# Layer 0 scoring of a two-layer graph network: one gather per super-tile of 256 edges instead of one per visit

## The reference, cut to what matters

```
key_e = k_rel[edge_type, edge_src]
val_e = v_rel[edge_type, edge_src]
att = (q[edge_dst] * key_e).sum(-1) * rel_pri[edge_type] / sqrt(64)
seg = edge_dst * 6 + edge_type
w   = exp(att - segment_max(att, seg)) / segment_sum(..., seg)
hsum = segment_sum(w[:, :, None] * val_e, seg)
```

## Time and profile before

| | |
|---|---|
| device time, median of 3 runs | 4169.86 us (4167.93 to 4179.78) |
| profiled execution, first to last instruction | 4487.9 us, 50605 instructions |
| busy in the profiled execution | DVE 2869.6, PE 2636.7, POOL 2419.6, ACT 1640.2 us |
| TensorE clock granted, mean | 0.779 |
| scoring with its gathers, 569.5 to 1907.6 us | 1338.1 us |
| rest of scoring, 1907.6 to 2114 us | 206.4 us |
| sum of messages, 2114 to 2604.5 us | 490.5 us |

### The profile page before, as it was taken

The page is one execution under the profiler, slowest core; times in us unless marked ns, Lnnn a source line. Parts: engine busy times, 40 slices in busy tenths (PEclk is TensorE's granted clock), DMA queues, the critical chain, the costliest instruction groups (busy, mean ns, idle before and its releaser), DMA issues. The chain is left out here.

```text
span 4487.9 us, 50605 instructions
## 1 busy us (share of the span) xinstructions
PE 2636.7 (59%) x10364; PEld 1802.2 (40%) x10365; DVE 2869.6 (64%) x5456; ACT 1640.2 (37%) x4268; POOL 2419.6 (54%) x2361
## 2 busy tenths in 40 slices
PE   0499845555656565612888867734555546555553
PEld 0255423333333333302666655523444434443442
DVE  4544434578777877895888866634555555555557
ACT  2244322333433433341444435422333333333343
POOL 4322266677677667701444444446666666666651
PEclk9999967766676766655999989966776777777776
DMA  6366698888888888804777721134555555555552
GB/s 202 126 257 256 266 288 267 260 265 262 258 261 267 252 266 262 258 24 141 234 238 234 237 63 35 33 70 138 161 168 162 168 159 166 167 160 167 162 150 92
DMA packets 607757, 852.98 MB, mean 190 GB/s; under 512 B 158649, under 2 KB 501445, under 8 KB 600987
## 3 DMA queue, kind: packets, MB, share of 16 engines
q0 software_dynamic: 128272, 451.36, 32.6%
q1 hardware_dynamic: 466614, 386.90, 27.4%
q10 hardware_dynamic: 12686, 12.72, 0.9%
HBM read 560.70 MB, written 291.24 MB: 190 GB/s over the span
## 5 line engine op out<-in xcount | busy, mean ns | idle before, releaser
L1051 POOL DMA_INDIRECT rows<-kv,kvi x880 | 930.8, 1058 | 425.8 <-issue 256.4
L2224 POOL DMA_INDIRECT g_rows<-x1t,srci x880 | 842.1, 957 | 474.8 <-issue 240.6
L1127 PE MATMUL psD<-qs,hot 128*128 x1760 | 695.3, 535 | 497.5 <-issue 263.2
L1127 PEld LDWEIGHTS psD<-qs,hot 128*128 128x128 f32 x1760 | 418.8, 263 | 727.6 <-issue 671.0
L2378 PE MATMUL g_psM<-g_rows,g_hot 128*128 128x264 f32 x1760 | 622.4, 513 | 63.7 <-issue 31.8
L1339 DVE TENSOR_TENSOR prod<-rows,psD 128x512 f32<-128x512 f32 x440 | 300.2, 682 | 390.9 <-DMA hsort<-hrow,tposi 197.5
L2378 PEld LDWEIGHTS g_psM<-g_rows,g_hot 128*128 128x128 f32 x1760 | 423.6, 253 | 177.1 <-issue 76.8
L1211 ACT ACTIVATE off<-psB,npiota 128x256 f32<-128x256 f32 x440 | 206.7, 470 | 746.2 <-DMA hsort<-hrow,tposi 294.0
L1715 PE MATMUL psM<-wv,vhot 128*128 128x260 f32 x1760 | 430.7, 393 | 82.0 <-ACT wv L1664 58.5
L1715 PEld LDWEIGHTS psM<-wv,vhot 128*128 128x128 f32 x1760 | 322.7, 191 | 189.9 <-issue 81.4
L1634 POOL TENSOR_TENSOR wv<-vrows,wgt 128x1024 f32<-128x1024 f32 x110 | 231.8, 2107 | 285.7 <-DVE vhot L1743 210.8
(11 more groups left out here) (447 smaller groups left out, 4446.2 us busy)
## 6 DMA issues: line engine op xcount, KB each, us to landing
val_v<-rows SPq DMA_DIRECT2D x220, 512.0 KB
vrows<-val_v SPq DMA_DIRECT2D x220, 512.0 KB
sums_v<-g_run SPq DMA_DIRECT2D x110, 528.0 KB
g_drow<-drow_v SPq DMA_DIRECT2D x55, 512.0 KB
rows<-kv,kvi POOLq DMA_INDIRECT x880
g_rows<-x1t,srci POOLq DMA_INDIRECT x880
xs<-in_x ACTq DMA_DIRECT2D x12, 896.0 KB, 10.3
g_ndt<-nodeb SPq DMA_DIRECT2D x440, 6.0 KB
```

Source lines behind the costliest of these rows:

```text
L1051: nc.gpsimd.indirect_dma_start(out=rows[:, k], out_offset=None, in_=table, in_offset=bass.IndirectOffsetOnAxis(ap=index[:, i * SLOTS + k:i ...
L1127: nc.tensor.matmul(psD[:, 2 * (V % 2) + j, 0:D], hot[:, V % 2, j * P:(j + 1) * P], node[:, ds(blk[V % 4], 1)].rearrange("p o d -> p (o d)" ...
L2224: nc.gpsimd.indirect_dma_start(out=rows[:, i % NBUF, k, 0:ROW1], out_offset=None, in_=dr["x1t"], in_offset=bass.IndirectOffsetOnAxis(ap=v[ ...
```

## The change

The gathers and the value stores go by super-tile instead of by visit, in layer 0's scoring alone.

- `kvi` holds 784 columns of indices (two per super-tile), made from the sorted edges and no longer from the visits' records, which lose that field. POOL issues 784 gathers, two super-tiles (a *pair*, four slots) at a time: 196 pairs.
- The ring keeps 16 slots, now eight super-tiles. A visit finds its super-tile's seat by a register: DVE reads `seat_e` and `need_e` for four visits at a time (two register loads, eight assertions on the second one), waits until `need_e` pairs have arrived, and takes `rows` at the register's offset.
- SP counts the arrived pairs (`arrived`), stores the pair's values (196 stores), and two pairs later waits until the last visit of that pair is done, by a number read from `past_e`; then it counts it as free (`freed`). POOL waits for `freed` in place of `prod_done`. So POOL's pair n waits until pair n - 2 has landed.
- The transfers of the flags and of the scores out and back move from SP's loop to ACT's; the softmax steps start a tick later (LAG = 3).
- `sum_messages` loads each visit's two slots with a transfer of its own, from the super-tile's place: 440 transfers of 256 KB in place of 220 of 512 KB, with the block numbers read to registers.
- `prepare_edges` gains the steps that make the three tables, and SP's record stores fall from 24 to 20.

```diff
@@ edge_weights, POOL
-                for i in range(NI):
-                    for g in range(SLOTS // GS):
-                        if i:
-                            pool.wait_ge(prod_done, (i - 1) * (SLOTS // 2) + (g + 1) * (GS // 2))
-                            pool.wait_ge(kept[g], 16 * i)
-                        for k in range(g * GS, (g + 1) * GS):
...
+                for n in range(NG):
+                    i, g = divmod(n, GE)
+                    if i:
+                        pool.wait_ge(freed, n - GE + 1)
+                        pool.wait_ge(kept[g], 16 * i)
+                    for k in range(GS):
...
@@ edge_weights, SP
-                for n in range(NTICK):
-                    i, g = divmod(n, SLOTS // GS)
+                for n in range(NG):
+                    i, g = divmod(n, GE)
                     for k in range(g * GS, (g + 1) * GS):
                         sp.wait_ge(got[k], 16 * (i + 1))
+                    sp.sem_inc(arrived, 1)
                     o = dr["val"].rearrange("(i k p) d -> i p k d", k=GS, p=P)[n]
                     sp.dma_start(o, rows[:, g * GS:(g + 1) * GS, D:2 * D]).then_inc(kept[g], 16)
-                    if n % PT == PT - 1:
-                        flags(n // PT)
-                    if n >= PT and n % PT == 1:
-                        hand_over(n // PT - 1)
-                hand_over(NQ - 1)
+                    m = n - 2
+                    if 0 <= m < NG - GE:
+                        if m % 4 == 0:
+                            past = nc.values_load_multi_w_load_instructions(v["past_e"][0:1, m:m + 4], ...)[1]
+                        sp.wait_ge(prod_done, past[m % 4])
+                        sp.sem_inc(freed, 1)
@@ edge_weights, ACT
+                        if n % PT == PT - 1:
+                            flags(n // PT)
+                    if n >= PT and n % PT == 2 and n // PT <= NQ:
+                        scores_out(n // PT - 1)
+                    if n >= PT and n % PT == 3 and n // PT <= NQ:
+                        scores_in(n // PT - 1)
@@ edge_weights, DVE
-                    dve.wait_ge(got[k], 16 * (i + 1))
-                    dve.wait_ge(got[k + 1], 16 * (i + 1))
+                    if V % 4 == 0:
+                        dve.load(seats, v["seat_e"][0:1, V:V + 4])
+                        needs = nc.values_load_multi_w_load_instructions(v["need_e"][0:1, V:V + 4], ...)[1]
...
+                    dve.wait_ge(arrived, need_of[V % 4])
                     dve.wait_ge(dst_done, 2 * V + 2)
                     if V >= 2:
                         dve.wait_ge(sc_done, V - 1)
-                    tt(prod[:, b:b + 2], rows[:, k:k + 2, 0:D], psD[:, b:b + 2, 0:D], ALU.mult).then_inc(prod_done, 1)
+                    tt(prod[:, b:b + 2], rows[:, ds(seat_of[V % 4], 2), 0:D], psD[:, b:b + 2, 0:D], ALU.mult).then_inc(prod_done, 1)
@@ sum_messages, SP
+                        if g % 2 == 0:
+                            sp.load(regs, v["blk"][0:1, ds(i * V8 + 2 * g, 4)])
                         sp.wait_ge(wv_done[g % 2], i * (NG // 2) + g // 2 + 1)
-                        o = dr["val"].rearrange("(i k p) d -> i p k d", k=GS, p=P)[ds(i * NG + g, 1)]
-                        sp.dma_start(rows[:, g * GS:(g + 1) * GS], o.rearrange("o p k d -> (o p) k d")).then_inc(loaded[g], 16)
+                        for u in range(2):
+                            at = nc.s_assert_within(
+                                i * V8 + (2 * g + u) - sp.snap(regs[2 * (g % 2) + u], min_val=0, max_val=NB - 1), 0, NS - 1, ...)
+                            k = g * GS + 2 * u
+                            sp.dma_start(rows[:, k:k + 2], values[ds(at, 1)].rearrange("o p k d -> (o p) k d")).then_inc(loaded[g], 16)
```

More of the change, by code:

```diff
@@ L19 @@
 NT = NV // VT
+RE = 8
 NC = 2 * NV
@@ L36 @@
 EPS = 1e-5
+ROUND = 1.5 * 2.0 ** 23
 SLOPE = 0.2
@@ L410, in prepare_edges @@
         b128 = sb("b128", [P, VT])
-        rv = sb("rv", [P, VT, NF, SUP])
+        rv = sb("rv", [P, VT, NR, SUP])
         dq = sb("dq", [P, VT, SUP])
+        cmps = va[:].rearrange("p t s -> p (t s)")[:, 0:NS]
+        parts, whole, supf = (a[0:1].rearrange("p t s -> p (t s)")[:, 0:NV] for a in (va, vb, dq))
+        past = cmp[0:1, 0:NS]
         vrow = sb("vrow", [P, 3, VT, SUP], BF16)
@@ L559, in _, with whole_of @@
                 step(nc.vector.tensor_copy(v["blk"][:], bfull[0:1, :]))
+                step(nc.vector.scalar_tensor_tensor(out=past, in0=psum[0:1, 3, 64:64 + NS], scalar=1.0, in1=viota[0:1, 0:NS], op0=ALU.add, op1=ALU.add))
+                dve.wait_ge(s_pad, 16 * PADS)
+                step(nc.vector.tensor_copy(v["past_e"], past.rearrange("o (n k) -> o n k", k=2)[:, :, 1]))
                 step(tsc(b128[0:NT], bvt[0:NT], float(P), None, ALU.mult))
+                step(tt(supf, viota[0:1, :], bfull[0:1, :], ALU.subtract))
+                def whole_of(n):
+                    step(tsc(parts, supf, 1.0 / n, (n - 1) / (2.0 * n), ALU.mult, ALU.subtract))
+                    step(tsc(whole, parts, ROUND, None, ALU.add))
+                    step(tsc(whole, whole, ROUND, None, ALU.subtract))
+                for n, ring, seats, needs in ((2, RE, v["seat_e"], v["need_e"]),):
+                    whole_of(n)
+                    step(tsc(needs, whole, 1.0, None, ALU.add))
+                    whole_of(ring)
+                    step(nc.vector.scalar_tensor_tensor(out=parts, in0=whole, scalar=-float(ring), in1=supf, op0=ALU.mult, op1=ALU.add))
+                    step(tsc(seats, parts, 2.0, None, ALU.mult))
                 dve.wait_ge(s_got, 64)
@@ L956 @@
 NTICK = NI * (SLOTS // GS)
-STEPS, LAG = 43, 2
+STEPS, LAG = 43, 3
+NG = NS // 2
+GE = RE // 2
 PB = R // 2
@@ L1208, in _, with piece_rows, flags, scores_out @@
             def _(act):
+                def piece_rows(name, q):
+                    return dr[name][q * GR * PL:(q + 1) * GR * PL].rearrange("(g s) -> g s", s=PL)
+                def flags(q):
+                    if q:
+                        act.wait_ge(flags_free, q)
+                    for h in range(H):
+                        act.dma_start(fi[h * GR:(h + 1) * GR], piece_rows("first", q)).then_inc(f_in, 16)
+                        act.dma_start(la[h * GR:(h + 1) * GR], piece_rows("last", q)).then_inc(f_in, 16)
+                def scores_out(q):
+                    for n in range(2):
+                        t = 2 * q + n
+                        act.wait_ge(tr_out, t + 1)
+                        act.dma_start(dr["att"].rearrange("h (t c p) -> t c h p", c=PC, p=P)[t], stage[:, n]).then_inc(att_put, 16)
+                def scores_in(q):
+                    act.wait_ge(att_put, 32 * (q + 1))
+                    for h in range(H):
+                        act.dma_start(w[h * GR:(h + 1) * GR, q * PL:(q + 1) * PL],
+                                     dr["att"][h, q * GR * PL:(q + 1) * GR * PL].rearrange("(g s) -> g s", s=PL)).then_inc(a_in, 16)
                 def places(V):
@@ L1645, in _ @@
                     sp.dma_start(win[:, t % 2], weights.rearrange("h (t c p) -> t c h p", t=CT, p=P)[t]).then_inc(w_in[t % 2], 16)
+                regs = [sp.alloc_register(f"ssup{t}") for t in range(4)]
+                values = dr["val"].rearrange("(s k p) d -> s p k d", k=2, p=P)
                 with sp.Fori(0, NI) as i:
                     for g in range(NG):
+                        if g % 2 == 0:
+                            sp.load(regs, v["blk"][0:1, ds(i * V8 + 2 * g, 4)])
                         sp.wait_ge(wv_done[g % 2], i * (NG // 2) + g // 2 + 1)
[L1650 to L1651 removed]
+                        for u in range(2):
+                            at = nc.s_assert_within(
+                                i * V8 + (2 * g + u) - sp.snap(regs[2 * (g % 2) + u], min_val=0, max_val=NB - 1), 0, NS - 1,
+                                skip_runtime_bounds_check_because="a visit lies its block's number past its super-tile, of which there are NS")
+                            k = g * GS + 2 * u
+                            sp.dma_start(rows[:, k:k + 2], values[ds(at, 1)].rearrange("o p k d -> (o p) k d")).then_inc(loaded[g], 16)
                 sp.wait_ge(x_back, 16 * XG)
```

80 lines of the change are left out of this document (42 added, 38 removed).

## The result

The changed kernel takes 4205.39 us (median of 4 runs, 4203.37 to 4212.32) beside 4174.82 us for the kernel before (4167.93 to 4182.14). The ratio is 1.0079, 95% interval 1.0063 to 1.0096: 31 us slower, where 78 us faster was forecast.

A forecast was written before the change was run, and what follows sets the result against it. The prediction took POOL's gathers in scoring as the bound, with DVE late next. It summed -120 + 28 + 6 + 5 + 3 = -78 us, so 4170 became 4092 us, range 4020 to 4150.

The forecast's parts named there:

- The bound: Scoring, before the change: POOL has work for 89% of the stage, 1187 of 1338 us in gathers and gaps.
- the upper bound of 128 us: Scoring: most that a late DVE could give back, the time it already waits for PE by name.
- The rival in which the products set the pace: Scoring: the PE, ACT and DVE chain needs 3.04 us per visit whatever the gathers do; 4230 us, slower; chance 0.10.
- Removing 96 gathers, -120: POOL's queue in scoring: 96 gathers fewer at 1.25 us each, gap included, save 120 us.
- the 28 forecast: Scoring's four parts with softmax steps: DVE, last by 11 us, and POOL starve each other; 28 us given back.
- The surplus of the mean gather over the median: POOL's gathers in scoring: 96 us in all, said to follow DVE's work and to stay after the change.
- DVE's register work, 37 us of need: DVE in scoring: 110 four-visit blocks showing 0.22 us each and 440 visit instructions showing 0.03 us each.
- The cover: DVE in scoring: 0.68 of the 0.90 us of register work every fourth visit lies under the reduction ahead.
- ACT +6, the sum of messages +5, preparation 0: ACT's transfers in scoring cost 6 us, extra loads in the sum of messages 5, preparation's added DVE steps nothing.
- POOL's landing wait, +3, 0 to 40: POOL in scoring: two pairs in flight allow 4.7 us per pair, under POOL's 5.0; scatter costs 3 us.
- The rival on landing: POOL in scoring: pairs landing 6 us after their last gather take 5.85 us each; about 4150 us; chance 0.11.
- the third: DVE's register loads in scoring take 0.6 us each, about 46 us more given back; 4138 us; chance 0.06.

The follow-up runs named there:

- the stretched profile: The kernel before, unchanged, in the first profile, which the prediction used; the profiled execution spans 4487.9 us.
- the second profile: The kernel before, unchanged, profiled again; the execution spans 4168.2 us.
- the kernel with both edits: The changed kernel with constants in place of DVE's register work in scoring, and SP counting pair n - 1 as free, not n - 2; 4080.80 us, ratio 0.9776.
- constants against registers: The changed kernel with DVE's seats and counts as program constants, so no register loads, assertions or register instructions in scoring; 4102.30 us, ratio 0.9842.
- the earlier count: The changed kernel with SP counting pair n - 1 as free, not pair n - 2, so three pairs can be on their way; 4197.09 us, ratio 1.0070.
- the last kernel above: The changed kernel with one eight-value load and no assertions on DVE, load and register instructions behind two products, pair n - 1 counted free; 4100.86 us, ratio 0.9836.
- the smaller block: The changed kernel with one load of eight values and no assertions on DVE, in one piece at the same place; 4149.32 us, ratio 0.9959.

## Why the prediction was wrong, step by step

**The bound: right, but DVE's waits were misread.** POOL set the pace before the change, and more clearly than the earlier trace rows of the stretched profile let one see. The prediction took PE's product for the likeliest cause of DVE's 325 us of waits there; in the second profile they are 236 us, 205 of them for rows and 29 for PE. So the upper bound of 128 us, taken from waits that bore PE's name, had no ground. The rival in which the products set the pace named the right sign for the wrong reason: the stage is as long as before with POOL idle, as it said, but PE is hardly late in either kernel (29 and 52 us ahead of DVE's products). The warning sign, a profiled execution 318 us longer than the timed one, was told and then set aside.

**Removing 96 gathers, -120 with DVE late next: near in size, in part by luck.** Alone it gives -97, so 23 us do not arrive, without any register work. That these lie near the 28 forecast is luck: the 28 were for a DVE with 37 us of register work, and without it the prediction's own sum leaves DVE at 833 + 21 = 854 us in the four parts, below POOL's 873. The even spread over the pieces was wrong too (6 to 39 gathers per piece: block borders, at which a super-tile is visited twice, lie closer together late in the list). Most of the removed gathers lie where DVE is nearly full; the first piece, where it has room, takes 214 us with the change's gathers and 199 with an even spread (the two rows of the kernel with both edits), and the other four give back 10 of these 15 us.

The surplus of the mean gather over the median was laid to DVE, not to the gathers. In piece 5 it is 184.09 - 169 x 0.949 = 23.7 us before and 145.21 - 130 x 0.946 = 22.2 after: 23% fewer gathers, 6% less surplus. "SBUF — State Buffer" of the Trainium skill has a cause for this in its section on the ports: while DVE runs an operation in a mode that takes the port pair which it shares with GpSimd, GpSimd cannot write its descriptors. The trace agrees by these two numbers; which of DVE's instructions hold the gathers up no run here tells.

**DVE's register work, 37 us of need: the step that failed.** It measured some 100 us of the kernel's time (constants against registers: 103 between the medians, 97 when each is set against its own kernel before), and 116 with the earlier count. Both factors of the sum 110 x 0.22 + 440 x 0.03 that stood for the time which shows were too small, and so was the price ahead of them.

*The price of an assertion.* The earlier trace rows took a checked value at the 0.018 us of its assertion. In the trace of before, the row between the load and the assertion on the same line showed that each checked value has a register instruction of its own:

```profile
L892 PEldq FUSED_REGOPS  x7: 151/151/175, 182.8 to 537.1; - x7
```

In the changed kernel, on DVE:

```profile
L1387 DVEq TENSOR_LOAD <-blank x110: 339/345/1362, 564.6 to 1803.4; - x110
```

```profile
L1388 DVEq FUSED_REGOPS  x440: 183/186/223, 565.4 to 1805.0; - x147
L1388 DVEq SEQ_ASSERT  x440: 23/23/41, 565.7 to 1805.3; - x147
L1388 DVEq TENSOR_LOAD <-blank x110: 336/342/1204, 565.0 to 1803.8; - x110
```

That is 0.345 + 0.342 + 4 x (0.186 + 0.023) = 1.52 us per four visits, and 2.03 in the median of the 110 blocks from the start of the first load to the end of the last register instruction, where 0.90 was put; the "eight assertions" of the order were four of these pairs.

*The cover.* 0.68 us was to lie under the reduction and 0.22 to show. DVE's queue does run ahead, and on the whole it hid more than 0.68: in the 88 blocks of the four pieces with softmax steps the trace has 201 us of block, and 84 us of it lie behind the end of DVE's last instruction. But that is 0.95 us per block that shows, in place of 0.22. It is uneven, too: 20 of the 88 leave no idle time ahead of their product, 65 leave more than 0.3 us. One of these:

```profile
1205.26 0.89 DVE L1422 SCALAR_TENSOR_TENSOR xs<-xs 128x704 f32<-128x704 bf16 x1
1207.55 0.69 DVE L1396 TENSOR_TENSOR prod<-rows,psD 128x512 f32<-128x512 f32 x1 [1.40 <-issue]
```

The block starts with the softmax step at 1205.26 and outlasts it: 1.40 us of idle time.

*Each visit's own register instruction.* 0.03 us of it was to show. In the changed kernel it shows at nearly every second visit, where the product stands directly behind a reduction: these are the 49 us, 0.11 per visit. With constants that line is gone; in the last kernel above, with the smaller block in two parts and the earlier count, it is still there:

```profile
  DVE early L1379: 51.6, 210
```

No run removes this instruction alone, so its share in the 20 us between that kernel (4100.9) and the one with constants and the earlier count (4080.8) stays open.

*The place of the cost.* DVE's need in the four parts with softmax steps was put at 884 us. The four pieces take 1009 us in the changed kernel (255.5 + 254.4 + 252.3 + 247.0); with the earlier count they take 1012 us, and 904 without the register work. POOL could do no more than DVE let it.

**ACT +6, the sum of messages +5, preparation 0: small, as forecast.** With the block out of the way all of them together, and SP's counting, leave 2 us on balance; they were not measured one by one. The 6.5 us of the sum of messages in the changed kernel do not come back in the kernel with constants and the earlier count, whose loads are the same, so they are no price of the loads; what they are stays open.

**POOL's landing wait, +3, 0 to 40: right in kind, small in size.** It measured 2 to 8 us beside the block, not clear of noise, and 21 us without it. The rival on landing asked for 6 us per pair. By the prediction's own sum landing already delays POOL above 4.3 us, where (4.7 + 4.3 + 1)/2 reaches POOL's 5.0; the 3.6 us of the earlier trace rows was one pair. In the changed kernel SP's store goes 4.0 us behind a pair's last gather in the median, but later than 4.3 us for 77 of the 196 pairs, which is enough to delay a count now and then.

**The nearest rival** was the third, DVE's loads being slow. It had the place, a chance of 0.06, and 46 us more where the runs show some 100: its price was the loads' time alone, and the loads were as fast as the trace of before had them. "DMA: Bandwidth & Descriptors" of the Trainium skill, section on latency, puts the floor of a load at about 600 ns. The trace differs: it shows 345 ns for four values and 601 for eight. What a late DVE takes back, forecast at 28 us with bounds of 0 and 128, adds up to 23 + 103 = 126 us with the change's count and 23 + 116 = 139 with the earlier one: at the upper bound or past it. The range of the whole did not reach even to that bound.

## What to carry to other kernels

An engine that is second by a few per cent has no room for work "beside": price every instruction that is put into its queue, registers and checks too, by all rows of the line that shows such a load, and let the range go as far as the bound of that term. When a wait on a count grows, ask who makes the count late before widening the count: here some 100 of the 176 us that POOL waited for SP were DVE's. And when the profiled execution is much longer than the timed one, take a second profile before anything else.

## What the runs showed of the hardware that was not expected

A register load from SBUF on DVE takes longer for more values: 345 ns for four, 601 ns for eight. A checked value costs 0.186 + 0.023 us on DVE. In the block shown above DVE's queue hid such work only under the instruction ahead of it; over the 88 blocks of four pieces it hid 117 of 201 us. The smaller block of 0.95 us cost the kernel some 25 us less when it was cut in two and put behind two products.
